# Graph attention twice over: seeds for the first steps of two chunks, taken from later steps

## The reference

```python
scores = (Wh @ a1)[:, None] + (We @ a2)[None, :]     # layer 0, slope 0.2
e = where(scores > 0, scores, ALPHA * scores)
attention = softmax(where(adj > 0, e, NEG_BIG), axis=1)
x = layernorm(x + elu(attention @ entity_embs + x))
# layer 1: wh = x @ weight_w; the same scores, slope 0.01, softmax over adj
x = layernorm(x + (attention @ wh + bias))
```

## Time and profile before

| | |
|---|---|
| median of 3 runs | 618.26 us (618.02 to 618.95) |
| profiled execution: its time | 618.98 us |
| its span, first to last instruction | 617.2 us |
| busy: VectorE, ScalarE | 553.6 us (90%), 545.3 us (88%) |
| busy: TensorE, GpSimd | 500.9 us (81%), 180.6 us (29%) |
| mean granted TensorE clock | 0.983 |

### The profile page before, as it was taken

One profiled execution on the slowest core, in us unless ns is written; L12 is line 12 of the kernel. 1 busy time (PEld: TensorE's weight loads), 2 busy tenths in 40 slices (PEclk: granted clock), 3 DMA queues, 4 the chain that ended last, 5 costly groups with the idle time before them and its releaser, 6 DMA issues.

```text
span 617.2 us, 14340 instructions
## 1 busy us (share of the span) xinstructions
PE 500.9 (81%) x6037; PEld 232.8 (38%) x6039; DVE 553.6 (90%) x808; ACT 545.3 (88%) x632; POOL 180.6 (29%) x105
## 2 busy tenths in 40 slices
PE   1317678999989799999988786789889888989894
PEld 1214344433443334433345442343233332433352
DVE  4999999999899998989989879979988998889795
ACT  1879999899999998899989989989998999888784
POOL 1081100465027650177001001005620742034051
PEclk9999989989999999999999999979999999999998
DMA  9998995965667745550100010010000001000001
GB/s 206 383 379 329 342 337 208 326 219 196 238 207 275 261 150 240 160 208 1 37 19 2 2 36 1 3 35 2 1 22 23 1 2 31 6 1 9 12 2 27
DMA packets 21341, 76.17 MB, mean 123 GB/s; under 512 B 10412, under 2 KB 11612, under 8 KB 13084
## 3 DMA queue, kind: packets, MB, share of 16 engines
q1 hardware_dynamic: 20472, 74.89, 34.9%
q0 software_dynamic: 112, 0.28, 0.2%
q10 hardware_dynamic: 692, 0.08, 0.1%
HBM read 74.16 MB, written 1.09 MB: 122 GB/s over the span
## 4 chain that ended last, share of the span: by engine, by line
DVE 36%; issue 27%; ACT 19%; PE 15%; POOL 2%; DMA 1%; POOLq 0%; ACTq 0%; DVEq 0%
DVE junk L972 17%; ACT Pm L840 14%; PE acc L1287 8%; DVE zps L1168 7%; PE zps L1349 5%; ACT zps L832 3%; DVE v L949 2%; PE acc L1294 1%; POOL rstd L644 1%; DMA acol<-in_L_gnn_a 1%; ACT v L698 1%; DVE D L992 1%; DVE X L1062 0%; DVE tot L1041 0%; POOL tAB L590 0%
## 5 line engine op out<-in xcount | busy, mean ns | idle before, releaser
L840 ACT ACTIVATE Pm<-zps,ebias 128x1024 f32<-128x1024 f32 (+1 forms) x320 | 292.1, 934 | 26.1 <-DVE zps L1168 22.3
L832 ACT ACTIVATE zps<-S_row,ntau_col 128x1024 f32<-128x1024 f32 (+1 forms) x216 | 205.8, 958 | 5.5
L1349 PE MATMUL zps<-D,v 128*128 128x128 bf16 x2048 | 165.1, 223 | 40.6 <-ACT zps L832 26.9
L1349 PEld LDWEIGHTS zps<-D,v 128*128 128x128 fp8e4 x2048 | 118.1, 99 | 181.8 <-ACT zps L832 85.3
L1287 PE MATMUL acc<-Pm,VE 128*32 128x512 f32 (+2 forms) x1280 | 146.4, 530 | 19.7 <-ACT Pm L840 14.8
L972 DVE CUSTOM_DVE_ANT_0 junk<-v,u_row 128x2048 int8<-128x2048 int8 x64 | 155.3, 2439 | 0.2
L972 DVE CUSTOM_DVE_ANT_0 junk<-v,adj_in 128x2048 int8<-128x2048 int8 (+3 forms) x88 | 155.4, 1803 | 0.0
L1287 PE MATMUL acc<-Pm,X 128*32 128x512 f32 (+2 forms) x1280 | 139.0, 522 | 18.9 <-ACT Pm L840 17.3
L1168 DVE SCALAR_TENSOR_TENSOR zps<-S_row,tau_col,zps 128x1024 f32<-128x1024 f32 (+1 forms) x104 | 106.1, 1043 | 34.9 <-PE zps L1349 34.4
L1294 PE MATMUL acc<-Pm,ones 128*32 128x256 f32 (+1 forms) x1280 | 86.6, 343 | 0.0
L573 POOL TENSOR_TENSOR tAB<-flag,totW 128x520 f32<-128x520 f32 (+1 forms) x7 | 12.9, 1842 | 219.4 <-PE zps L1349 114.8
(11 more groups left out here) (175 smaller groups left out, 249.9 us busy)
## 6 DMA issues: line engine op xcount, KB each, us to landing
adj_in<-in_adj SPq DMA_DIRECT2D x62, 1024.0 KB, 5.4
S_row<-S_rows_scratch SPq DMA_DIRECT2D x6, 512.0 KB, 4.0
Pm<-in_adj SPq DMA_DIRECT2D x2, 1024.0 KB, 9.5
VE<-in_L_gnn_entity_embs SPq DMA_DIRECT2D x2, 512.0 KB, 5.6
S_row<-S_rows_scratch SPq DMA_DIRECT2D x3, 256.0 KB, 3.2
out<-tAB SPq DMA_DIRECT2D x3, 256.0 KB, 2.6
adj_in<-u_row_scratch SPq DMA_DIRECT2D x2, 256.0 KB, 3.1
S_row<-S_rows_scratch POOLq DMA_DIRECT2D x1, 256.0 KB, 8.1
```

The source lines that it names most:

```text
L832: a.activation(mask_of(n), S_row[:, C % 2, 0:R(C) * P], ACT.Relu, bias=ntau_col[:, layer(C), n % JT:n % JT + 1]).then_inc(seed_done, 1)
L840: a.activation(Pm_of(k, 0, R(C) * P), mask_of(k), ACT.Exp, bias=ebias[:, layer(C), int(seeded(k)), J:J + 1])\
L1349: last = t.matmul(mask[:, r * P:(r + 1) * P], v[:, chunks[C][1] + r, J * P:(J + 1) * P], D[:, C % 2, PART * second + r, :], start=(r * P % ...
```

## The change

It does four things.

- In chunks 7 and 8 the steps 0, 1 and 2 may be seeded (`across` is true for every chunk of layer 1 but the last).
- Seeds of chunks 7, 8 and 9 may be issued from two steps before the chunk begins (`first`), which makes 7.0 and 7.1 stand before the exponentials of 6.30 and 6.31, and 8.0 and 8.1 before those of 7.30 and 7.31. ScalarE waits for that chunk's S_row there. Chunk 9 has no seeds.
- `WITHOUT` makes steps 3, 12, 18 and 29 of chunk 7 and steps 3, 10 and 17 of chunk 8 unseeded. Chunk 7 then has 20 seeded steps and chunk 8 has 11.
- In chunks 7 and 8 the first two maxima stand in steps 0 and 2, instead of 3 and 4 (chunk 7) and 3 and 6 (chunk 8).

```diff
-               7: (7, 10, 15, 20, 22, 25, 27),
-               8: tuple(J for J in range(JT) if J not in (3, 6, 9, 10, 13, 16, 17, 19, 23, 26, 29))}
+               7: (3, 7, 10, 12, 15, 18, 20, 22, 25, 27, 29),
+               8: tuple(J for J in range(JT) if J not in (0, 1, 2, 6, 9, 13, 16, 19, 23, 26, 29))}
...
-            across = C != LAST and (narrow(C) or narrow(max(C - 1, 0)))
+            across = C != LAST and (C > NC or narrow(C) or narrow(max(C - 1, 0)))
...
-            seeds_from = max(seeds_from, JT * C, free, k - min(seed_ahead(C), J // 2 + 1))
+
+            first = JT * C - SEED_AHEAD * (C > NC + 1)
+            seeds_from = max(seeds_from, first, free, k - min(seed_ahead(C), J // 2 + 1 + JT * C - first))
...
             first = MAXIMA_FROM if layer(C) else 1
-            return [(nxt, i // 2, i % 2) for i in range(n) if first + i * (JT - 2 - first) // n == J]
+            steps = [first + i * (JT - 2 - first) // n for i in range(n)]
+            if layer(C):
+                steps[0:2] = 0, 2
+            return [(nxt, i // 2, i % 2) for i in range(n) if steps[i] == J]
...
                     for n in seeds_at.get(k, []):
+                        if n // JT > C:
+                            wait_S(act, n // JT)
                         wait_buf(act, "step", n)
-                        a.activation(mask_of(n), S_row[:, C % 2, 0:R(C) * P], ACT.Relu,
+                        a.activation(mask_of(n), S_row[:, n // JT % 2, 0:R(n // JT) * P], ACT.Relu,
                                      bias=ntau_col[:, layer(C), n % JT:n % JT + 1]).then_inc(seed_done, 1)
```

## The result

The changed kernel takes 624.35 us in the median of six runs (623.55 to 625.73), against 619.58 us for the kernel before in six runs (618.02 to 621.05). The ratio is 1.008 with a 95% interval of 1.0059 to 1.0101. Of 619.58 us that is 5.0 us, between 3.7 and 6.3; the two medians are 4.8 us apart. The profiled execution took 624.63 us with a span of 622.8.

What follows compares the result with a forecast made beforehand. VectorE was taken to set the pace between the turns, ScalarE in chunk 7's tail. Shifts of +4.1 at exponential 7.25 and +1.2 in the tail, +5.3 after chunk 8, on median 618.26 gave 623.5; range 622.3 to 625.6.

Steps and rivals of the forecast that it cites:

- Turn into chunk 7: Start of chunk 7: three early seeds delay exponential 7.0 to 467.76, and correction 7.5 comes 1.43 us later.
- Chunk 7: From correction 7.5 to exponential 7.25: VectorE's longer list brings the shift at exponential 7.25 to +4.1 us.
- The two corrections: Chunk 7, new corrections 12 and 18 on VectorE before 7.25: +2.40 us.
- The small term: Chunk 7, correction 18 waits for its mask, at 499.95 instead of 499.7: +0.25 us.
- Tail: From exponential 7.25 to 8.0, ScalarE sets the pace with two more seeds: +1.2 us more, exponential 8.0 +5.3.
- Chunk 8: Exponential 8.3 +6.2 us; new corrections 10 and 17 use up VectorE's waits, leaving +5.3 at correction 18.
- carried to the end: From correction 18 of chunk 8 on, both orders are the same, so the +5.3 us shift stays to the end.
- GpSimd: No change taken for maxima held up by GpSimd; bounds 1.7 us less, 1.2 more; rival of freed maxima 621.8, chance 0.11.
- The rival that ScalarE sets the pace: VectorE takes the added corrections for nothing: 616.9 us, or 614.6 if the turns also cost nothing; chance 0.13.
- The rival that the turns pay: VectorE's 3.20 us wait before 8.0 swallows its longer list: 618.3, or up to 621 if partly; chance 0.10.
- VectorE's gapless stretch: Chunk 7: from correction 7.5 at 474.21, VectorE has no wait for a mask until that of 8.0.

Runs made afterwards that it cites:

- kernel with one early seed: Kernel before with only step 0 of chunks 7 and 8 seeded early, a maximum moved into correction 0's place in each: +1.22 us by the stretch, ratio 1.0041.
- the turn by itself: Kernel before with early seeds for 7.0, 7.1, 7.2 and maxima at 0 and 2, no step of chunk 7 unseeded, chunk 8 unchanged: +2.36 us, ratio 1.0046.
- two maxima fewer: The change with two more maxima of chunk 7 early (at 0, 1, 1, 2; none at 14 and 24): +2.69 us against the kernel before, ratio 1.0040.
- the maximum in the wait of 3.20 us: Kernel before with chunk 9's first maximum taken in step 31 of chunk 7, none at step 13 of chunk 8: -1.21 us, ratio 0.9988.
- chunk 7 only: Kernel before with only chunk 7's part of the change, chunk 8 as before: +3.13 us by the stretch, ratio 1.0052.
- the maxima back: The change without the lines that move the first two maxima: +9.98 us by the stretch against the kernel before, ratio 1.0172.

## Why the prediction was right, point by point

Forecast 623.5, measured 624.35 in the median; forecast shift 5.3, measured 4.8 between the medians and 5.6 between the two spans, of which 4.86 lie in the stretch that the change touches. The forecast was 0.85 too low in the time and 0.4 too high in the shift: it started from a median of 618.26 in three runs, and that of all six is 619.58.

- **Turn into chunk 7**: exponential 7.0 forecast at 467.76, measured 468.72 - 0.76 = 467.96. Correction 7.3: 472.34 against 472.24. Correction 7.5: 475.64 against 475.73, so +1.52 for +1.43. VectorE's wait: 5.4 against 5.21. The mechanism is right; that 7.3 came out within 0.1 is in part luck. The three seeds took 0.2 more than forecast, and from the projection to the mask of 7.3 there were 0.99 us where 1.16 were taken. The chain also has a step that the forecast left out: the mask of 7.4 waited 0.32 us for its seed.
- **Chunk 7**: exponential 7.25 at 517.6 against 518.33 - 0.76 = 517.57. From correction 7.5 to exponential 7.25 it is 2.56 more, of 2.65 forecast. The two corrections were worth 2.34 of their 2.40 (489.90 to 491.05 and 500.75 to 501.94), in keeping with the kernel that adds only these. The small term was mis-ascribed: I had correction 18 wait 0.25 for its mask, but it has no wait. The 0.24 is in the maximum at 493.26, which took 3.36 us with GpSimd's operation in its way, where its counterpart before took 3.12.
- **Tail**: exponential 8.0 at 531.9 against 532.11; from exponential 7.25 on +1.42 for +1.2. Each seed at a turn cost some hundredths more than 1.17: it starts about 0.1 behind the end of the exponential ahead of it (529.55 behind 528.36 and 1.09), where other seeds start 0.03 behind (525.06 behind 523.93 and 1.10). No run shows why.
- **Chunk 8**: exponential 8.3 at 538.1 against 537.71; maximum 9 at 545.65 against 545.46; behind it the waits of 1.60 and 0.84 were used up as forecast (+5.24 at correction 18). Here one step was wrong: from correction 18 on I said that the shift is carried to the end. It was 5.24 there and 4.86 at the diagonals of chunk 9, for the most part because the kernel before has a wait of 0.26 before correction 22 that the later order does not have. The term was 0.4 too large.
- **GpSimd**: three maxima of chunk 7 were held up before and three after, none was freed, and maximum 9 won its race again (2.28 us at 546.22). Two operations of GpSimd did run free beneath the new corrections, 1.04 us instead of about 3:

```profile
490.06 1.04 POOL L591 TENSOR_TENSOR o<-o,rden 128x512 f32<-128x512 f32 x1 [2.45 <-DVE rden L625]
491.18 3.29 POOL L596 TENSOR_TENSOR tAB<-o,X 128x512 f32<-128x512 f32 x1
```

But GpSimd's second operation, 491.18 here, stopped the next maximum each time. I had taken nothing for all this, and it is the 0.24 above. The Trainium skill's rule of the exclusive lock (SBUF — State Buffer, "Who interferes with whom") fits the rows, but the freeing that it allows did not come. The kernel with one early seed has 3.12 us for that maximum, and 3.36 once 7.12 is unseeded too; that the second operation is the reason was read from the timeline and not tried by a run.

- **The rival that ScalarE sets the pace** fell with two kernels: three seeds more made the change 1.6 us faster, two seeds fewer made the kernel before 2.6 slower. **The rival that the turns pay** needed exponential 8.0 no later than 526.6; it came at 532.11, and the turn by itself is +2.36.

One thing behind the forecast stood on weaker ground than it seemed: that VectorE's gapless stretch begins at 7.5. It made no difference to the change, whose added corrections are at 12 and later, but it spoiled the forecast of the kernel with one early seed. The prediction also says that ScalarE waits once in that stretch; its own rows have a second wait there, 0.37 us at 475.53, which enters no term.

## What to carry to other kernels

A wait at a seam between stages is not room for any work of the engine that waits: work put ahead of an operation that another engine's next step needs moves that step back, so ask for each filler who reads what comes behind it. When two engines are both over 90% busy, look for the one without waits over tens of microseconds and count the list that stands inside its gapless stretch. Here the time went with what entered or left that list, two corrections more for 2.58 us, until waits opened elsewhere (two maxima fewer gave 2.2 of 4.4). Fill a seam on the engine that waits longest in it, with work that nothing in the seam waits for, as the maximum in the wait of 3.20 us did: 1.21 us by the stretch, though the timed runs are too coarse to confirm it.

## What the runs showed of the hardware

While ScalarE waited 3.15 us for correction 7.20, TensorE stood idle for 2.65 us, and in this execution its granted clock fell afterwards. The busy times and the granted clock by stretch, after the change (PE, PEld, DVE, ACT, POOL, clock):

```profile
500.00:506.00 6.00, 5.95 (x68) 2.43 (x64) 5.97 (x8) 5.31 (x5) 4.12 (x2) 1.00 0.01 4
506.00:512.00 6.00, 3.35 (x29) 1.11 (x22) 6.00 (x7) 3.42 (x4) 0.00 (x0) 0.77 0.00 0
510.00:511.00 1.00, 1.00 (x8) 0.00 (x0) 1.00 (x3) 1.00 (x2) 0.00 (x0) 0.50 0.00 0
```

The next product and mask ran at the lower level:

```profile
509.68 1.94 PE L1295 MATMUL acc<-Pm,X 128*32 128x512 f32 x8 [2.65 <-ACT Pm L848]
511.55 1.03 PE L1357 MATMUL zps<-D,v 128*128 128x128 bf16 x8
```

against 1.06 and 0.62 us just before. A granted clock of 0.50 is half speed, 1.2 of 2.4 GHz. It does not follow on every such wait. Four kernels have it at this step: with two corrections more for the kernel before a product took 1.93 us, one step later; with chunk 7 only, and with the maxima back, the product behind the same 2.65 us took 1.06 and 1.07, at a granted clock of 1.00. With chunk 7 only:

```profile
508.09 1.06 PE L1295 MATMUL acc<-Pm,X 128*32 128x512 f32 x8 [2.65 <-ACT Pm L848]
```

What decides between the two is not shown. The slow product and mask cost this kernel nothing: the kernel with chunk 7 only did not have them, and its diagonals of chunk 8 stand 64.62 us behind those of chunk 7, as after the change. The mask of correction 7.22 had been written ahead of the idle time, and 7.25, the next correction, had no wait.
